# Codebook search with one fp32 matmul per unit, and depthwise taps as diagonal matmuls on TensorE

## The chip, the cores and the metric

The kernel runs on one core of a Trainium2 chip, in one launch. The metric is the device time in microseconds (us), lower is better. One core has TensorE (PE, matmuls into PSUM), VectorE (DVE), ScalarE (ACT), GpSimd (POOL) and SyncE (SP), which run their own instruction streams and wait for each other by semaphores. TensorE's clock is granted at one of two levels, 1.2 or 2.4 GHz; the profile shows which, as a share of full speed.

## The reference

The input x is 2 images of 128 channels and 48x48 pixels. Four layers each add to it: `x = x + layer(_gn(x))`, where `_gn` normalizes groups of 4 channels.

```python
# layer 0: guidance conv 3x3 -> softmax weights of 5x9 dilated taps -> 1x1 conv -> batch norm
# layer 1: nearest code of each pixel vector z among 8192 codes of 128 values
d = jnp.sum(z_flat ** 2, axis=1, keepdims=True) + jnp.sum(codebook ** 2, axis=1) - 2.0 * jnp.matmul(z_flat, codebook.T)
z_q = codebook[jnp.argmin(d, axis=1)]
# layer 2: depthwise 3x3 conv, its 9 taps of each image and channel computed from the pooled image
kern = jax.nn.relu(x.mean(axis=(2, 3)) @ Wk.T + bk)
out = lax.conv_general_dilated(xr, kern, ..., feature_group_count=b * c)
# layer 3: two deformable 3x3 convs (offset conv, gather of 4 corners of 9 taps, mix), each with group norm and relu
```

All in fp32. The channels lie on the 128 partitions.

## The kernel before

The program has these stages.

*Opening and guidance* (functions `Opening`, `guidance`): load x, normalize it into the padded image `xpad`, then for six rounds of 8 rows each a 3x3 conv on PE (`conv`, line 417), a softmax on DVE (lines 506 to 520), and transposes to and fro (`turn`, `turn_back`). Beside it, class `CodeSplit` loads the transposed codebook in 8 groups of 128x1024 fp32 through two buffers (SP, line 956), and POOL splits each into a bf16 high part (line 962) and a bf16 rest (line 964). The guidance block ends when all engines have done their part.

*Branches* (`branches`): the 45 dilated taps of layer 0, with DVE multiplying, PE and POOL adding.

*Between*: scalars of the two norms on DVE in a chain of small steps, then the first 512 pixels z of layer 1 as fp32 (line 886, DVE), as bf16 high (line 906, ACT) and as bf16 rest (line 888, DVE). PE starts the search when both are there. POOL then makes the other 4096 pixels, in fp32, high and rest (lines 917 to 934), and the second chunk of the search waits for it (`rest`, `DONE`).

*Search* (`search_steps`, `step`): 9 chunks of 512 pixels (n = 0 to 8), each in 4 steps (s), each of 16 units (k). A unit is the scores of 512 pixels against 128 codes: three bf16 matmuls of 128x512 into one PSUM bank (high x high, high codes x low z, low codes x high z; lines 1431 to 1433). Units 0 and 1 of a step are copied out by ACT with a bias (line 1593). Units 2 to 15 are taken by DVE, which keeps a running maximum (line 1864). The scores have 5 banks in turn (`SLOT`), so PE can be at most 4 to 6 units ahead of the engine that empties them. After units 9 and 11 PE transposes the running maxima of the step before (`turn`, line 1335), and once per chunk z (`turn_z`) and the chosen codes (`turn_zq`). For the chunk before, DVE finds the best blocks (`find`, `place_block`, at unit 12 and 14 of step 0 and at six units of step 1), POOL gathers candidates and multiplies, ACT sums, DVE picks, POOL fetches the codes and adds.

In the last three chunks further work is put between the units by the tables of the functions `lead`. At chunk 6 (`L0`), image 0 has its layer-1 result: DVE takes its moments (step 0, unit 10), PE makes the 9 tap weights of each channel (`pe_kernels`, line 220), ACT normalizes the image into `xpad` (`applied`), and DVE adds the nine taps to x with one full-image instruction each (`tap`, line 254) at nine units of steps 2 and 3, then takes the moments of the result. Chunks 7 and 8 prepare the first deformable job of image 0.

*First job* (`first_job`): the end of the search for the last chunk, then the same depthwise for image 1, with DVE doing 18 half-image taps (`half_tap`, line 264), nine for each half, with `weigh(0, 2, 4)` between the halves. In between, PE and ACT go on with tiles 2 to 4 of job 0, whose corners ACT multiplies (`product`, line 1634), while DVE's next tile is tile 5, behind `norm(1)`.

*Jobs*: 4 jobs (2 convs, 2 images) of 18 tiles of 128 pixels. For each tile POOL issues 9 indirect DMAs (`rows`, line 2076) that gather the corners into one of 5 buffers. `rows(T)` waits until PE has turned tile T-5 (`turn_done`). DVE weighs the corners (lines 1909 to 1919), PE turns (line 1458) and mixes (line 1469). The order on each engine is written out by hand, and every queue works in that order.

Of the kernel before, what the change touches and what calls it, by code (L numbers as in the profile page):

```python
# [15 lines left out]
P = 128  # L16
B, H, W = 2, 48, 48
# [7 lines left out]
ROWS = 8  # L25
# [164 lines left out]
class Depthwise:  # L190
# [5 lines left out]
    def __init__(self, tools, ctx, a, x, xpad, gm32):  # L196
# [10 lines left out]
        self.done = [tools.sem(ctx, "tap_done") for _ in range(B)]  # L207
# [34 lines left out]
    def dve_kernels(self, dve, b, ps):  # L242
        dve.wait_ge(self.kern_ready, b + 1)
        self.norm.chained(dve, dve.tensor_tensor(self.kern[:], ps[:, 2:2 + TAPS], self.bk[:], ALU.add))
        self.norm.chained(dve, dve.tensor_scalar(self.kern[:], self.kern[:], 0.0, None, ALU.max))
        dve.wait_ge(self.applied, b + 1)

    def tap(self, dve, b, k):
        v = self.xpad[:, b * PADDED:(b + 1) * PADDED].rearrange("p (r w) -> p r w", w=WP)
        v = v[:, k // 3:k // 3 + H, k % 3:k % 3 + W]  # L250
        xb = self.x[:, b, :].rearrange("p (r w) -> p r w", w=W)
        if k:
            dve.wait_ge(self.done[b], k)
        dve.scalar_tensor_tensor(xb, v, self.kern[:, k:k + 1], xb, ALU.mult, ALU.add).then_inc(self.done[b], 1)

    def half_tap(self, dve, b, h, k, sums):
        v = self.xpad[:, b * PADDED:(b + 1) * PADDED].rearrange("p (r w) -> p r w", w=WP)
        v = v[:, h * H // 2 + k // 3:h * H // 2 + k // 3 + H // 2, k % 3:k % 3 + W]
        xb = self.x[:, b, h * HW // 2:(h + 1) * HW // 2].rearrange("p (r w) -> p r w", w=W)
        sums = sums.rearrange("p (r w) -> p r w", w=W)  # L260
        n = TAPS * h + k
        if n:
            dve.wait_ge(self.done[b], n)
        dve.scalar_tensor_tensor(sums if k < TAPS - 1 else xb, v, self.kern[:, k:k + 1], sums if k else xb,
                                 ALU.mult, ALU.add).then_inc(self.done[b], 1)
# [101 lines left out]
def guidance(nc, tools, xpad, w_guide, ident, ident_b, a_sel, b_sel, wta, wtb, opening, beside):  # L367
# [5 lines left out]
    with ExitStack() as ctx:  # L373
# [387 lines left out]
def layer0(nc, tools, a, x, xpad, gm32, gm8, ident, codes, y, stats, xy, moments, gb, between):  # L761


    with ExitStack() as ctx:
# [3 lines left out]
        with ExitStack() as ctx:  # L768
# [9 lines left out]
            ch, cl, nc2, code_rows = codes  # L778
            with ExitStack() as parts:
                guidance(nc, tools, xpad, w_guide, ident, ident_b[:], (sel_a, id3a), (sel_b, id3b), wta, wtb,  # L780
                         Opening(tools, parts, x, xpad, gm32, moments, loads), CodeSplit(nc, tools, parts, a, ch, cl))
# [15 lines left out]
class Between:  # L797
# [6 lines left out]
    def __init__(self, tools, ctx, x, y, stats, xy, moments, gb, gm32):  # L804
# [14 lines left out]
        self.affine = tools.sem(ctx, "z_affine")  # L819
        self.high = tools.sem(ctx, "first_high")  # L820
        self.low = tools.sem(ctx, "first_low")
# [13 lines left out]
    def dve(self, dve, ps, each, z, zh, zl):  # L835
# [49 lines left out]
        dve.sem_inc(self.affine, 1)  # L885
        chain(dve.tensor_scalar(z, first, scale[:, 0:1], self.first_shift[:, 0:1], ALU.mult, ALU.add))
        dve.wait_ge(self.high, 1)
        dve.tensor_tensor(zl, z, zh, ALU.subtract).then_inc(self.low, 1)
# [3 lines left out]
    def pe(self, pe, ps):  # L892
# [4 lines left out]
        pe.wait_ge(self.high, 1)  # L897
        pe.wait_ge(self.low, 1)

    def act(self, act, zh):  # L900
# [4 lines left out]
        act.wait_ge(self.affine, 1)  # L905
        act.activation(zh, self.x[:, 0:self.FIRST], ACT.Identity, bias=self.first_shift[:, 0:1],
                       scale=self.scale[:, 0:1]).then_inc(self.high, 1)

    def pool(self, pool, early, places):
# [6 lines left out]
        pool.wait_ge(self.high, 1)  # L916
# [6 lines left out]
        for a, c, b in cuts:  # L923
            z, zh, zl = places(a, c)
            pool.tensor_scalar(z, x[:, a:c], self.scale[:, b:b + 1], self.shift[:, b:b + 1], ALU.mult, ALU.add)\
                .then_inc(rest, 1)
        pool.wait_ge(rest, 6)
        for a, c, b in cuts:
            z, zh, zl = places(a, c)
            pool.tensor_copy(zh, z).then_inc(rest, 1)  # L930
        pool.wait_ge(rest, 9)
        for a, c, b in cuts:
            z, zh, zl = places(a, c)
            pool.tensor_tensor(zl, z, zh, ALU.subtract).then_inc(rest, 1)

    DONE = 12


class CodeSplit:


    SLOTS = 2

    def __init__(self, nc, tools, ctx, a, ch, cl):
        self.a, self.ch, self.cl = a, ch, cl
        self.ct = tools.sb(ctx, "codes_t", [P, self.SLOTS, PER * P])
        self.ct_in = [tools.sem(ctx, "codes_t_in") for _ in range(self.SLOTS)]
        self.high = tools.sem(ctx, "high_ready")
        self.low = tools.sem(ctx, "low_ready")

    def sp(self, sp):
        for g in range(GROUPS):
            s = g % self.SLOTS
            if g >= self.SLOTS:
                sp.wait_ge(self.low, g - self.SLOTS + 1)
            sp.dma_start(self.ct[:, s, :], self.a["codes_t"][:, g, :]).then_inc(self.ct_in[s], 16)

    def pool(self, pool):
        for g in range(GROUPS):
            s = g % self.SLOTS  # L960
            pool.wait_ge(self.ct_in[s], 16 * (g // self.SLOTS + 1))
# [1272 lines left out]
```

## Time and profile before

| | us |
|---|---|
| median of 3 runs | 1657.97 (1655.91 to 1658.62) |
| the profiled execution, its own time | 1659.29 |
| its span, first to last instruction | 1657.5 |

| engine | busy us | share of the span |
|---|---|---|
| PE | 1207.6 | 73% |
| DVE | 1359.2 | 82% |
| ACT | 430.0 | 26% |
| POOL | 1009.7 | 61% |

The guidance fills the first 85 us of the span, the branches end at about 306, the search runs from 319 to 820, and the jobs fill the rest. The chain of work that ended last is mostly POOL (25% of the span, all in line 2076) and its issue time. In the rows below a start and a duration are in us; a grouped row ends with busy us, the mean of one in ns, and idle us before it; "x36" is the number of instructions merged into one row; a bracket behind a row is the idle time of the engine before it and what ended that. A duration of a matmul includes its latency, so the pace of a stream is read from distances of starts. An fp32 matmul has two instructions, and so two records, where a bf16 matmul has one.

### The profile page before, as it was taken

Reading aid. Unit: us, or ns where it says so; the run is one execution under the profiler, and the core shown is the slowest. Engines: PE = TensorE matmul, PEld = TensorE weight load, DVE = VectorE, ACT = ScalarE, POOL = GpSimd, SP = SyncE. Lnnn points to the kernel's source line nnn. Section 1 sums busy time; section 2 is a strip of 40 time slices with the busy share of each in tenths; the row PEclk is TensorE's granted clock in tenths of the full one; section 3 lists DMA queues with packets and bytes.
Section 4 is the critical chain, followed back from the end, with each engine's and each line's share of the span. In section 5 each row is a group of like instructions: output and inputs, shape, how many; then the busy total and the mean of one; then the engine's idle time right before and its main releaser. Section 6 shows DMA issues by size and latency. Waiting matters only on the chain. (4 is left out here: it accounts for less than half of the span.)

```text
span 1657.5 us, 19707 instructions
## 1 busy us (share of the span) xinstructions
PE 1207.6 (73%) x5997; PEld 747.5 (45%) x6040; DVE 1359.2 (82%) x1885; ACT 430.0 (26%) x1354; POOL 1009.7 (61%) x977
## 2 busy tenths in 40 slices
PE   5889989698889987689857685676665566555554
PEld 2455555354444444244336454544444444444443
DVE  5568678789999999989967889987887777797775
ACT  1241000124333443243457231221112212111111
POOL 6158578444333443235777677777777777777772
PEclk9889999899999999789978797697777778767677
DMA  4051000012111121053476796787877878777773
GB/s 168 13 166 40 1 0 0 15 31 58 53 43 34 46 58 39 20 153 107 142 225 201 216 288 208 211 267 229 247 209 228 248 229 247 211 232 212 208 210 99
DMA packets 111101, 232.64 MB, mean 140 GB/s; under 512 B 14676, under 2 KB 60500, under 8 KB 110748
## 3 DMA queue, kind: packets, MB, share of 16 engines
q0 software_dynamic: 58176, 191.30, 39.0%
q1 hardware_dynamic: 52828, 40.17, 7.7%
q8 instruction: 46, 0.75, 0.2%
q14 instruction: 51, 0.42, 0.1%
HBM read 205.15 MB, written 26.26 MB: 140 GB/s over the span
## 5 line engine op out<-in xcount | busy, mean ns | idle before, releaser
L2076 POOL DMA_INDIRECT code_region<-corners,lead_region x252 | 240.9, 956 | 77.9 <-issue 75.8
L1864 DVE SCALAR_TENSOR_TENSOR max_region<-score,nc,max_region 128x512 f32<-128x512 f32 x324 | 230.5, 740 | 28.4 <-PE score L1433 26.2
L742 POOL TENSOR_TENSOR prod_acc<-prod_acc,prod_pool 128x752 f32<-128x752 f32 (+8 forms) x112 | 151.8, 1355 | 98.1 <-DVE prod_pool L715 90.6
L2076 POOL DMA_INDIRECT early_region<-corners,lead_region x136 | 129.0, 948 | 41.3 <-issue 40.8
L1458 PE MATMUL score<-ident,code_region 128*128 128x128 f32 x540 | 96.9, 340 | 77.6 <-DVE code_region L1913 73.0
L2076 POOL DMA_INDIRECT max_region<-corners,lead_region x130 | 124.1, 955 | 39.6 <-issue 38.7
L2076 POOL DMA_INDIRECT late_region<-corners,lead_region x126 | 119.9, 951 | 44.6 <-issue 37.8
L1864 DVE SCALAR_TENSOR_TENSOR max_region<-lead_score,nc,max_region 128x512 f32<-128x512 f32 x180 | 132.2, 741 | 8.1 <-PE lead_score L1433 7.6
L1458 PEld LDWEIGHTS score<-ident,code_region 128*128 128x128 f32 x540 | 78.6, 176 | 94.8 <-DVE code_region L1913 87.5
L1991 POOL DMA_INDIRECT late_region<-code_rows,block_id x35 | 37.0, 1058 | 135.3 <-DVE block_id L1706 98.7
L664 PE MATMUL y_ps<-prod_pe,w_scale 128*128 128x384 f32 (+9 forms) x396 | 107.6, 397 | 0.0
L1909 DVE TENSOR_TENSOR lead_score<-lead_score,code_region 128x768 f32<-128x768 f32 x78 | 75.3, 966 | 37.0 <-DMA code_region<-corners,lead_region 33.8
L715 DVE TENSOR_TENSOR prod_pool<-spread,xpad 128x752 f32<-128x752 f32 (+8 forms) x112 | 81.9, 739 | 26.1 <-PE spread L641 25.3
L2003 POOL TENSOR_TENSOR late_region<-late_region 128x1032 f32<-128x1032 f32 x32 | 72.6, 2268 | 45.1 <-DMA late_region<-code_rows,block_id 44.4
L1530 ACT COPY max_region<-turn_ps 128x512 f32<-128x512 f32 x72 | 42.2, 586 | 202.3 <-PE turn_ps L1335 202.3
L1521 ACT ACTIVATE late_region<-late_region 128x129 f32<-128x129 f32 x280 | 82.5, 299 | 17.3 <-POOL late_region L2003 12.0
L641 PE MATMUL spread<-wta,sel_a 108*128 x352 | 74.7, 318 | 16.6 <-DVE prod_pool L715 6.6
L1641 ACT COPY code_region<-score 128x384 f32<-128x384 f32 x72 | 34.4, 478 | 191.2 <-PE score L1458 185.8
L1458 PE MATMUL score<-ident,early_region 128*128 128x128 f32 x292 | 50.2, 329 | 43.1 <-DVE early_region L1913 33.9
L1458 PE MATMUL score<-ident,late_region 128*128 128x128 f32 x252 | 48.6, 357 | 43.3 <-DVE late_region L1913 43.3
L715 DVE TENSOR_TENSOR prod_pe<-spread,xpad 128x768 f32<-128x768 f32 (+8 forms) x98 | 67.6, 698 | 14.8 <-PE spread L641 14.5
L1913 DVE TENSOR_TENSOR code_region<-lead_score,code_region 128x768 f32<-128x768 f32 x78 | 74.7, 957 | 2.7
(289 smaller groups left out, 3098.2 us busy)
## 6 DMA issues: line engine op xcount, KB each, us to landing
corners<-lead_region SPq DMA_DIRECT2D x72, 192.0 KB
corners<-lead_region SPq DMA_DIRECT2D x8, 576.0 KB
code_rows<-codes_n SPq DMA_DIRECT2D x8, 516.0 KB, 4.2
codes_t<-in_codes_t SPq DMA_DIRECT2D x8, 512.0 KB, 3.7
codes_n<-in_codes SPq DMA_DIRECT2D x8, 512.0 KB, 4.4
code_region<-corners,lead_region POOLq DMA_INDIRECT x252, 3.7
x<-in_x SPq DMA_DIRECT2D x2, 1152.0 KB, 6.3
out<-x SPq DMA_DIRECT2D x4, 576.0 KB, 3.3
```

Of the source, the lines that this page charges most:

```text
L641: mm = pe.matmul(to, sel[:, kk, :], v, start=True, stop=True)
L664: mm = pe.matmul(dst, w_scale[:, o["i"] + 1, :], src.rearrange("p (r w) -> p r w", r=rows), start=False, stop=last, skip_group_check=True)
L715: dve.tensor_tensor(to, w, v, ALU.mult).then_inc(prod_ready, 1)
L742: pool.tensor_tensor(to, to, v, ALU.add).then_inc(pooled, 1)
L1458: mm = pe.matmul(tps[g][:, k * P:(k + 1) * P], quad(T, 3 * g + k)[:, c * P:(c + 1) * P], ident, start=c == low, stop=c == CORNERS - 1, is_ ...
L1521: act.activation(v, v, ACT.Identity, accum_out=fine[:, u, j:j + 1]).then_inc(summed, 1)
L1530: act.copy(maxima[n % 2][:, :, g * P:(g + 1) * P], turn_ps[:]).then_inc(kept, 1)
L1864: dve.scalar_tensor_tensor(r, score[SLOT[k]], nc2[:, m:m + 1], r, ALU.add, ALU.max).then_inc(dve_took, 1)
L1909: return dve.tensor_tensor(upper_ps, bc(w[:, k, 0:2], P), q[:, k, 0:2], ALU.mult)
L1913: dve.tensor_tensor(q[:, k, 2:4], upper_ps, q[:, k, 2:4], ALU.add).then_inc(halved, 1)
L2003: pool.tensor_tensor(v, v, zb, ALU.mult).then_inc(multiplied, 1)
L2076: pool.indirect_dma_start(quad(T, k), None, table[j].rearrange("n s c -> n (s c)"), bass.IndirectOffsetOnAxis(index[j % B][:, at:at + 1], 0))\
```

## The change

1. The search has one fp32 matmul of 128x512 per unit in place of three bf16 ones. No high and low parts are made: `CodeLoad` loads the eight code groups straight into their place without POOL, `Between` makes z in fp32 alone, and POOL has 6 instructions in place of 12 before the second chunk.
2. The depthwise taps of both images are sums on PE: ACT makes nine diagonal 128x128 matrices from the tap weights (`act_diagonals`), and PE multiplies them with shifted windows of `xpad`, 9 matmuls of 128x384 per 8 rows, six such groups per image (`pe_taps`). DVE adds each result from PSUM to x.
3. For image 0 the groups of taps and their adds stand at units of steps 2 and 3 of chunk 6 (`TAPS_AT`, `ADDS_AT`). For image 1 PE does the groups of one half after `pe_kernels`, then tile 2, then those of the other half, then tiles 3 and 4; DVE has two adds of half an image.

```diff
+    def act_diagonals(self, act, b, ident, to):
+        act.wait_ge(self.kern_done, b + 1)
+        for k in range(TAPS):
+            act.activation(to[:, k * P:(k + 1) * P], ident, ACT.Identity, scale=self.kern[:, k:k + 1])\
+                .then_inc(self.diag_ready, 1)
+
+    def pe_taps(self, pe, b, r, diag, ps):
+        at = b * PADDED + r * (ROWS * WP)
+        for k in range(TAPS):
+            v = self.xpad[:, at + k // 3 * WP + k % 3:at + k // 3 * WP + k % 3 + ROWS * WP]
+            mm = pe.matmul(ps, diag[:, k * P:(k + 1) * P], v.rearrange("p (r w) -> p r w", w=WP)[:, :, 0:W],
+                           start=k == 0, stop=k == TAPS - 1)
+        return mm
...
-            beside.pool(pool)
...
-        pe.wait_ge(self.high, 1)
-        pe.wait_ge(self.low, 1)
-
-    def act(self, act, zh):
+        pe.wait_ge(self.first, 1)
+
+    def act(self, act):
...
+class CodeLoad:
...
     def sp(self, sp):
         for g in range(GROUPS):
...
+            sp.dma_start(self.codes[:, g, :], self.a["codes_t"][:, g, :]).then_inc(self.loaded, 16)
+        sp.wait_ge(self.loaded, 16 * GROUPS)
...
+    TAPS_AT = (0, 2, 1), (0, 2, 7), (0, 2, 13), (0, 3, 4), (0, 3, 9), (0, 3, 13)
+    ADDS_AT = (0, 2, 4), (0, 2, 10), (0, 3, 2), (0, 3, 7), (0, 3, 12), (0, 3, 15)
...
-                    pe.matmul(o, ch[g][:, w], high, start=True, stop=False)
-                    pe.matmul(o, ch[g][:, w], low_, start=False, stop=False)
-                    pe.matmul(o, cl[g][:, w], high, start=False, stop=True).then_inc(score_ready, 1)
+                    pe.matmul(o, codes_t[:, g, w], chunk_of(z_early, z_late, n), start=True, stop=True)\
+                        .then_inc(score_ready, 1)
...
                 depthwise.pe_kernels(pe, 1, dps)
-                for T in range(2, 5):
+                taps(0)
+                tile(0, 2 // TPC, 2 % TPC)
+                taps(1)
+                for T in range(3, 5):
                     tile(0, T // TPC, T % TPC)
...
                 depthwise.act_norm(act, 1)
+                depthwise.act_diagonals(act, 1, ident, diag1)
...
-                for t in range(2 * TAPS):
-                    if t == TAPS:
-                        weigh(0, 2, 4)
-                    depthwise.half_tap(dve, 1, t // TAPS, t % TAPS, tap_sums)
+                weigh(0, 2, 4)
+                for h in range(2):
+                    xh = x[:, 1, HALVES[h]].rearrange("p (c n) -> p c n", n=CH)
+                    dve.wait_ge(depthwise.tapped, NCH + h + 1)
+                    dve.tensor_tensor(xh, tap_sums, xh, ALU.add).then_inc(depthwise.done[1], 1)
```

`taps(h)` on PE waits for all nine diagonals, and for h = 1 for DVE's first add. Each group for image 0 waits in the same way for the add of the group before.

## Rows read from the trace of the kernel before

**Rows 1.** Timeline of PE in chunk 2 of the search: start, duration, engine, line, operation.

```profile
400.36 0.38 PE L1431 MATMUL lead_score<-early_region,code_region 128*128 128x512 bf16 x1
400.58 0.38 PE L1432 MATMUL lead_score<-early_region,code_region 128*128 128x512 bf16 x1
400.80 0.38 PE L1433 MATMUL lead_score<-early_region,code_region 128*128 128x512 bf16 x1
401.01 0.60 PE L1335 MATMUL turn_ps<-ident,max_region 128*128 128x128 f32 x4
401.45 0.38 PE L1431 MATMUL lead_score<-early_region,code_region 128*128 128x512 bf16 x1
```

**Rows 2.** PE timeline of fp32 matmuls, 256 and 384 columns; the latter's group.

```profile
872.45 1.46 PE L1469 MATMUL turn_ps<-max_region 128*128 128x256 f32 x6
...
304.56 1.48 PE L664 MATMUL y_ps<-prod_acc,w_scale 128*128 128x384 f32 x4
...
L664 PE MATMUL y_ps<-prod_acc,w_scale 128*128 128x384 f32 x96 | 35.9, 496 | 0.0
```

**Rows 3.** Timeline of ACT: its first units of steps 0, 1, 2 of chunk 2 and of chunk 3.

```profile
416.67 1.27 ACT L1593 ACTIVATE max_region<-lead_score,nc 128x512 f32<-128x512 f32 x2 [3.20 <-PE lead_score L1433]
428.34 1.28 ACT L1593 ACTIVATE max_region<-lead_score,nc 128x512 f32<-128x512 f32 x2 [2.06 <-PE lead_score L1433]
444.29 1.27 ACT L1593 ACTIVATE max_region<-lead_score,nc 128x512 f32<-128x512 f32 x2 [2.73 <-PE lead_score L1433]
...
467.75 1.27 ACT L1593 ACTIVATE max_region<-lead_score,nc 128x512 f32<-128x512 f32 x2 [3.15 <-PE lead_score L1433]
```

**Rows 4.** DVE: two units in the timeline; the finds of one chunk, grouped by line.

```profile
816.07 1.40 DVE L1864 SCALAR_TENSOR_TENSOR max_region<-score,nc,max_region 128x512 f32<-128x512 f32 x2
...
L1701 DVE MAX8 best<-max_region 128x8 f32<-128x1024 f32 x4 | 4.9, 1218 | 0.0
```

**Rows 5.** Chunk 0, chunk 6, its steps 2 and 3, chunk 7, chunk 8: busy time by engine.

```profile
320.50:365.55 45.05, 44.84 (x214) 21.87 (x217) 37.74 (x56) 8.76 (x14) 29.90 (x13) 0.98 0.11 29
621.01:696.82 75.81, 56.76 (x248) 28.11 (x252) 71.56 (x106) 22.26 (x83) 25.24 (x22) 0.87 0.12 32
655.86:696.82 40.96, 27.68 (x114) 12.75 (x116) 40.12 (x50) 11.91 (x56) 15.90 (x14) 0.84 0.12 33
696.82:765.28 68.46, 58.18 (x273) 27.95 (x277) 63.65 (x116) 27.74 (x92) 20.84 (x22) 0.89 0.36 104
765.28:820.20 54.92, 48.76 (x249) 23.32 (x252) 49.95 (x95) 20.46 (x82) 39.92 (x42) 1.00 0.45 133
```

The columns are window, its length, busy us and instructions of PE, weight loads, DVE, ACT and POOL, the granted clock, the DMA share and GB/s.

**Rows 6.** Line 254, the taps of image 0: min/median/max in ns, first and last start.

```profile
L254 DVE SCALAR_TENSOR_TENSOR x<-xpad,kern,x x9: 2605/2609/3879, 658.6 to 699.0; 128x2304 f32<-128x2304 f32 x9
```

**Rows 7.** Timeline of PE in the guidance.

```profile
42.09 0.26 PE L435 MATMUL wa_ps<-ident_b,w_split 128*108 128x128 bf16 x1 [3.79 <-DVE w_split L520]
...
44.99 8.05 PE L417 MATMUL g_ps<-xpad,w_guide 128*64 128x384 f32 x36
...
55.42 6.03 PE L417 MATMUL g_ps<-xpad,w_guide 128*64 128x384 f32 x36
```

**Rows 8.** Timeline ahead of the search, DVE.

```profile
318.18 0.69 DVE L888 TENSOR_TENSOR early_region<-early_region 128x512 bf16<-128x512 f32 x1 [0.32 <-ACT early_region L906]
```

**Rows 9.** Timelines of the first job: DVE, ACT, PE and POOL.

```profile
881.33 0.17 DVE L245 TENSOR_SCALAR kern<-kern 128x9 f32<-128x9 f32 x1
...
884.16 3.61 ACT L1634 ACTIVATE code_region<-code_region,lead_region 128x128 f32<-128x128 f32 x12
...
905.11 4.09 PE L1458 MATMUL score<-ident,max_region 128*128 128x128 f32 x36
...
914.06 0.59 PE L149 MATMUL z_ps<-n_mean_var,gm 128*128 128x2 f32 x2 [4.86 <-DVEq L144]
...
927.87 0.94 POOL L2076 DMA_INDIRECT late_region<-corners,lead_region  x1 [6.48 <-PE score L1458]
```

**Rows 10.** Waits of POOL from 822 us to the end: total us, times, longest.

```profile
POOL late_region L2076 <- PE score L1458: 6.8, 2, 6.5
```

More of the change, by code:

```diff
@@ L206, in __init__ @@
         self.applied = tools.sem(ctx, "applied")
-        self.done = [tools.sem(ctx, "tap_done") for _ in range(B)]
+        self.kern_done = tools.sem(ctx, "kernels_done")
+        self.diag_ready = tools.sem(ctx, "diagonals_ready")
+        self.tapped = tools.sem(ctx, "taps_summed")
+        self.done = [tools.sem(ctx, "taps_added") for _ in range(B)]
     def sp(self, sp):
@@ L243, in dve_kernels @@
         dve.wait_ge(self.kern_ready, b + 1)
+        if b:
+            dve.wait_ge(self.diag_ready, TAPS * b)
         self.norm.chained(dve, dve.tensor_tensor(self.kern[:], ps[:, 2:2 + TAPS], self.bk[:], ALU.add))
[L245 to L265, printed above, removed]
+        dve.tensor_scalar(self.kern[:], self.kern[:], 0.0, None, ALU.max).then_inc(self.kern_done, 1)
+    def act_diagonals(self, act, b, ident, to):
[10 more added lines that the diff above has]
+        return mm
 class Opening:
@@ L818, in __init__ @@
         self.group_rooted = tools.sem(ctx, "x_group_rooted")
-        self.affine = tools.sem(ctx, "z_affine")
-        self.high = tools.sem(ctx, "first_high")
-        self.low = tools.sem(ctx, "first_low")
+        self.first = tools.sem(ctx, "first_ready")
         self.shifts = tools.sem(ctx, "z_shifts")
@@ L884, in dve @@
         chain(dve.tensor_tensor(self.first_shift[:], self.first_shift[:], scale, ALU.mult))
[L885 to L888, printed above, removed]
+        dve.tensor_scalar(z, first, scale[:, 0:1], self.first_shift[:, 0:1], ALU.mult, ALU.add).then_inc(self.first, 1)
         chain(dve.scalar_tensor_tensor(self.shift[:], gmean, -1.0, scale, ALU.mult, ALU.mult))
@@ L1034, in code_views @@
 def code_views(region):
[L1036 to L1041 removed]
+    return region[:, 0:CODES].rearrange("p (g n) -> p g n", g=GROUPS)
 def finale(nc, tools, a, code_rows, x, xpad, ident, gm32, gm8, nc2, depthwise, between, places, out):
@@ L1404, in lead @@
                     depthwise.pe_kernels(pe, 0, lead_ps)
+                for r, when in enumerate(TAPS_AT):
+                    if at == when:
+                        pe.wait_ge(depthwise.applied, 1)
+                        pe.wait_ge(depthwise.diag_ready, TAPS)
+                        if r:
+                            pe.wait_ge(depthwise.done[0], r)
+                        depthwise.pe_taps(pe, 0, r, diag0, lead_ps[:, 0:CH]).then_inc(depthwise.tapped, 1)
                 if at == (1, 0, 3):
@@ L1471, in tile, with taps @@
                     mm.then_inc(mixed, 1)
+            def taps(h):
+                pe.wait_ge(pos_ready, 1 + NCH)
+                pe.wait_ge(depthwise.applied, 2)
+                pe.wait_ge(depthwise.diag_ready, 2 * TAPS)
+                if h:
+                    pe.wait_ge(depthwise.done[1], h)
+                for r in range(NCH // 2):
+                    mm = depthwise.pe_taps(pe, 1, h * NCH // 2 + r, diag1, tap_sums[:, r, :])
+                mm.then_inc(depthwise.tapped, 1)
             def first_job():
@@ L1686, in _ @@
             act.sem_inc(y_saved, 1)
-            between.act(act, zh_early[:, 0:PX])
+            between.act(act)
             search_steps(step)
@@ L1820, in lead @@
                     depthwise.dve_kernels(dve, 0, lead_ps)
-                for t, when in enumerate(((0, 2, 2), (0, 2, 3), (0, 2, 8), (0, 2, 13), (0, 2, 15),
-                                          (0, 3, 10), (0, 3, 11), (0, 3, 13), (0, 3, 14))):
+                for r, when in enumerate(ADDS_AT):
                     if at == when:
-                        depthwise.tap(dve, 0, t)
+                        xc_ = x[:, 0, r * CH:(r + 1) * CH]
+                        dve.wait_ge(depthwise.tapped, r + 1)
+                        dve.tensor_tensor(xc_, lead_ps[:, 0:CH], xc_, ALU.add).then_inc(depthwise.done[0], 1)
                 if at == (0, 3, 15):
-                    dve.wait_ge(depthwise.done[0], TAPS)
+                    dve.wait_ge(depthwise.done[0], NCH)
                     norm_.dve_moments(dve, x[:, 0, :])
@@ L1876, in norm @@
                 if j < 0:
-                    dve.wait_ge(depthwise.done[b], 2 * TAPS)
+                    dve.wait_ge(depthwise.done[b], 2)
                     norm_.dve_moments(dve, x[:, b, :])
```

73 lines of the change are left out of this document (19 added, 54 removed).

## The prediction

> **What bounds the kernel now.** I read the page's busy tenths first to see the stages, then for the search the starts of the steps and the paces of PE and DVE, then for the jobs the waits of POOL and the timelines around image 1's depthwise. Four stages matter.
>
> In chunk 0 of the search PE sets the pace. Three bf16 matmuls start 0.215 us apart, so a unit costs 0.647 us, and four transposes 0.44 us [rows 1]. A step of 16 units with two such turns is 16 x 0.647 + 0.88 = 11.23 us of PE, and chunk 0 took 45.05 us, 11.26 a step, with PE busy all but 0.2 us [rows 5]. In chunks 1 to 5 a chunk is 51.1 us (11.67 in step 0, 15.95 in step 1, 23.46 in the other two) [rows 3], while PE alone, with z and code transposes (0.88), would need 4 x 11.23 + 0.88 = 45.8. The missing 5.3 us lie at step 1: there DVE has its finds, 1.22 us each [rows 4], beside units that it takes at 0.66 us (two in 1.40, one's latency being 0.74) [rows 4]. So PE is 90% of the bound, and DVE the rest. Chunks 6 and 7 took 75.8 and 68.5 us with DVE busy 71.6 and 63.7 [rows 5]: there DVE's extra work is the bound.
>
> After the search POOL issues one gather every 1.25 us to the end. From 822 us on its waits for another engine in the main group sum to 6.8 us, nearly all one wait of 6.5 [rows 10]. So whatever holds POOL up in the first job moves the end by as much, and what speeds up PE or DVE there is worth at most those 6.5 us.
>
> **The change part by part.**
>
> *Unit of the search.* The trace has no fp32 matmul of 512 columns. With 256 columns six records take 1.46 us; with 0.38 for the last one's duration (that of the 512-column bf16 matmul [rows 1], which streams as many cycles) they are 0.216 apart, two records a matmul, 0.43 each. With 384 columns four records take 1.48: (1.48 - 0.50) / 3 = 0.33 apart, 0.65 a matmul [rows 2]. Both are four cycles a column at 2.4 GHz, with a new weight load each time that hides. So 512 columns cost 2 x 0.43 = 0.857 us, against 0.647: +0.21 us a unit. From 384 columns the same price comes to 0.65 x 512 / 384 = 0.87; I take 0.857, as the 256 columns are the cleaner stream, and keep 0.87 for the range. A step becomes 13.7 + 0.9 = 14.6 us of PE.
>
> The Trainium skill (TensorE: Matmul & The Clock Gate, Back-to-back issue gap) gives about 131 ns per 512-column matmul as the sustained pace in a stream with weight loads. The trace disagrees: 215 ns in exactly such a stream [rows 1]. By the page an fp32 unit of four passes would be an estimated 0.52 us, less than DVE's 0.66, and the first rival below would win.
>
> *Chunk 0:* 4 x 14.6 = 58.4, +13.4 us. POOL's six saved instructions there are worth nothing: it has a whole chunk for them.
>
> *Chunks 1 to 5:* PE needs 4 x 14.6 + 0.9 = 59.2 us. DVE's burst lasts from unit 12 of step 0 to unit 13 of step 1: 16 units x 0.66 and 8 finds at some 1.15 net, 19.8 us. PE's 18 units in it were 12.5 us and become 16.3. The difference falls from 7.3 to 3.5. The banks let PE run ahead some 2.0 us now (7.3 - 5.3), some 2.6 at slower units, so 1 us of stall remains; I take 1.2 (bounds 0 and today's 5.3). A chunk becomes 60.4, +9.3, five times +46.5 us.
>
> *Chunk 6:* DVE loses nine taps of 2.61 us (one 3.88) [rows 6], 24.8 us, and gets six adds of 384 columns. The trace has no such add; a unit's 0.66 for 512 columns [rows 4] bounds one from above and nothing from below, I take 0.55, 3.3 us, which decides nothing while PE is the bound. PE gets 54 matmuls of 0.65 to 0.66, 35.6 us. So the bound moves to PE: 59.2 + 35.6 + 2.5 (norm, kernels) = 97.3 us. The finds, moments and small steps of steps 0 and 1 keep DVE ahead as bound for a while; by the same reckoning as above PE stalls there some 4.4 us. 101.7 against 75.8: +25.9. Of that, the 41.0 us of steps 2 and 3 [rows 5] become 64 to 65. The diagonals are nine ACT instructions of 0.30 us (twelve in 3.61) [rows 9] in ACT's idle time; PE's first group can wait for them a us or so.
>
> *Chunk 7:* DVE no longer enters it late by two taps and the moments, and PE does 59.2 plus some 5 us of conv and transposes, with 1.3 of stall: 65.5 against 68.5, -3.0. *Chunk 8:* 59.2 + 2.6 + 1.8 = 63.6 against 54.9, +8.7. Together the search gets 13.4 + 46.5 + 25.9 - 3.0 + 8.7 = +91.5 us.
>
> *Guidance.* Without POOL's split DVE's first softmax rounds are no longer slowed, and PE's idle 3.8 us before the first turn back goes; the conv behind it, 8.05 us at a partly low clock where later ones take 6.03, and the turns beside it (1.0 us) run at full clock [rows 7]: 3.8 + 2.0 + 1.0 = -6.8. The later rounds are PE's own pace. The bounds are 0 and -9. The code loads now follow at once on the queue behind all others, which cost nothing by their place.
>
> *Before the search.* The rest of z and its wait are gone: -1.1 us (0.69 + 0.32 and a signal) [rows 8].
>
> *First job.* The tap weights are ready at 881.5 [rows 9]. ACT's diagonals take 2.7 us, PE's 27 matmuls 17.8, so tile 2 starts at 902 instead of 881, or 904 when the first matmuls run at the low clock after the wait. With tile 2's 4.1 us and 27 more matmuls taps(1) ends at 926. DVE's last add and the moments follow within some 5 us, 931; in the kernel before PE made that norm at 914.1 [rows 9]. But PE now stands before tiles 3 and 4. Tile 3 is turned by 930, tile 4 waits for ACT's products, which interleave with tile 3's copies (three times 3.61 [rows 9] and a copy of about half a us, from 926.5, so 939), and norm(1) follows on PE at 940.3: +26. DVE's tile 5 and then `rows(10)` on POOL, which started at 927.9 [rows 9], follow at that distance: 954. POOL's rows(8) and rows(9) in between wait too, but inside this. DVE loses its 18 half taps and gains nothing, since it waits. +26 us (bounds +14, if ACT's products were done early, and +45, if all 54 matmuls ran at half clock).
>
> *POOL's queue at the end of the search.* DVE's last picks lie 8 units before the end, which is 1.7 us longer now, so POOL has its fetches behind it that much earlier: -1.7.
>
> Sum against the profiled execution's 1659.3: 91.5 - 6.8 - 1.1 + 26 - 1.7 = +107.9, 1767.2. That execution lies 1.3 above the median of the runs, so I give 1766.
>
> **The rivals.**
>
> *DVE stays the bound of the search (faster).* It decides at the price of a unit: below (51.1 - 4.4) / 64 = 0.73 us, 0.365 a record, chunks 1 to 5 don't grow. For it speaks only that DVE is busy 82% of the span; against it, both fp32 widths in rows 2. At 0.52 a unit and taps scaled alike (0.39), the search loses some 20 us in chunk 6 and 5 in chunk 7, and the first job grows by some 8: 1659.3 - 7.9 - 20 - 5 + 8 = 1634. Chance 3%.
>
> *The stalls don't shrink.* If the finds cost PE the full 5.3 us a chunk with the longer units as well, chunks 1 to 5 get 4.1 each, chunks 6 and 8 some 3: +27, 1793. Against it: banks that hold longer units give more slack, not less. Chance 12%.
>
> *The clock falls in the taps.* In the first job PE waits before each half and the granted clock can be half for some of it, and around chunk 6's hand-overs too. Half of the 54 matmuls at 1.2 GHz cost 18 us more: 1784. Speaking for it: matmuls in streams with waits ran at the low clock in chunk 6 (0.84 mean) [rows 5]. Against: the taps are dense. Chance 10%.
>
> *The first job's delay is absorbed.* If POOL could catch up, +26 would vanish: 1740. Rows 10 show no slack to catch up with. Chance 6%.
>
> **How the numbers follow.** Forecast 69%, the others 3, 12, 10 and 6. The predicted time is the forecast's. Its own uncertainty is +-12: 3 for guidance, 6 for chunks 6 and 7, 6 for the stalls, 8 for the first job, and +8 at 0.87 us a unit (576 x 0.013). The range takes in the absorbed delay and the shrinking that fails, 1740 to 1793. A measurement of this kernel can tell 0.2%, 3.3 us, from no change. All cases but the first lie far above that: faster 0.03, same 0.01, slower 0.96.
>
> **What would show it.** In the changed kernel's trace: records of line 1431's successor 0.43 us apart; steps of 14.6 us in chunk 0; PE busy over 95% in chunks 1 to 5 with chunks of 60 us; chunk 6 near 102 us with DVE busy under 55; PE without the 3.8 us gap in the guidance, which ends near 78; norm(1) about 26 us later after the search's end than now, and POOL waiting there some 25 us more, with no other new wait. The prediction is wrong if a unit costs under 0.73 us, if chunks 1 to 5 come out at 64 or more, or if POOL regains time after the first job.

## The result and the profile after

| | before | after |
|---|---|---|
| median | 1658.3 us (1655.91 to 1658.77, 4 runs) | 1785.62 us (1783.28 to 1788.28, 4 runs) |
| the profiled execution, its own time | 1659.29 | 1783.28 |
| its span | 1657.5 | 1781.5 |

The ratio is 1.0768, with a 95% interval of 1.0755 to 1.0781: 7.7% slower, 127 us, where 108 were forecast. 1785.6 lies inside the range. The two spans differ by 124.0 us, and these are split below.

The page's first part for the kernel after, then the slices of 44.5 us each (busy tenths; PEclk is the granted clock):

```profile
PE 1386.8 (78%) x5680; PEld 834.3 (47%) x5680; DVE 1333.5 (75%) x1865; ACT 436.8 (25%) x1371; POOL 969.0 (54%) x955
...
PE   6899897999999999999984968666654765655554
...
DVE  4478677687888888368885178998788877878776
...
PEclk9899998999999999999997989768786887767666
```

PE gained 179 us of busy time, DVE lost 26. PE is at 9 from slice 8 to slice 20, nearly the whole search; DVE has a 3 (slice 17, in chunk 6, whose taps it gave away) and a 1 (slice 23, where it waits for PE in the first job).

The pace of a unit, in PE's timeline of chunk 0, as rows 1 showed it for before:

```profile
317.47 1.02 PE L1398 MATMUL score<-early_region,code_region 128*128 128x512 f32 x2
318.32 1.02 PE L1398 MATMUL lead_score<-early_region,code_region 128*128 128x512 f32 x2
319.18 1.02 PE L1398 MATMUL score<-early_region,code_region 128*128 128x512 f32 x2
```

A unit, two records, starts every 0.855 us, so 0.43 a record, twice the 0.216 that rows 2 gave for 256 columns. The stages in windows, with the columns of rows 5: chunk 0 (opened 1.1 us ahead of ACT's first unit, from which the table below counts it), chunk 1, chunk 6, its steps 2 and 3, chunk 7, chunk 8 with what follows its last score:

```profile
312.00:371.88 59.88, 59.88 (x155) 27.61 (x154) 42.04 (x56) 9.01 (x14) 18.55 (x7) 0.97 0.08 22
371.88:432.74 60.86, 59.74 (x169) 27.98 (x168) 51.07 (x81) 20.14 (x81) 18.56 (x20) 1.00 0.14 40
676.27:781.26 104.99, 100.73 (x297) 52.28 (x296) 57.93 (x106) 25.06 (x92) 20.89 (x22) 0.97 0.08 23
716.27:781.26 64.99, 64.21 (x191) 34.30 (x192) 23.91 (x47) 11.98 (x57) 10.33 (x12) 1.00 0.07 20
781.26:850.52 69.26, 65.44 (x213) 31.07 (x212) 59.24 (x112) 28.04 (x92) 20.86 (x22) 1.00 0.36 103
850.52:919.00 68.48, 64.55 (x200) 30.27 (x199) 55.24 (x95) 21.21 (x83) 43.21 (x46) 0.98 0.41 119
```

PE is busy all but 1.1 us of chunk 1 and all but 0.8 us of chunk 6's steps 2 and 3, where DVE has only 23.9 us of work left in 65. With the distances between ACT's first units (as rows 3), E for the end of the last score, and "jobs" for all that follows E in the span, the search of each kernel that was run comes out so (us):

| kernel | search starts | chunk 0 | 1 to 5, each | 6 | 7 | 8 | E | jobs |
|---|---|---|---|---|---|---|---|---|
| before | 319.4 | 45.1 | 51.1 | 75.8 | 68.5 | 54.5 | 819.7 | 837.8 |
| after | 310.9 | 58.8 | 60.9 | 105.0 | 69.3 | 66.2 | 916.8 | 864.7 |
| fp32 search alone | 310.4 | 58.8 | 60.9 | 78.2 | 77.5 | 66.3 | 897.7 | 840.8 |
| image 0's taps on DVE | 309.1 | 59.1 | 60.9 | 78.2 | 75.8 | 66.3 | 895.0 | 868.0 |
| image 1's taps on DVE | 310.0 | 58.7 | 60.9 | 105.0 | 69.7 | 66.6 | 916.5 | 840.1 |
| bf16 search, taps on PE | 320.0 | 45.1 | 51.1 | 95.9 | 65.3 | 54.4 | 837.8 | 866.3 |
| four bf16 a unit | 315.6 | 58.6 | 61.0 | 76.4 | 76.4 | 66.2 | 900.1 | 836.3 |
| two bf16 a unit | 319.6 | 37.6 | 47.7 | 73.4 | 68.2 | 52.5 | 790.9 | 843.0 |
| pauses in the split | 310.5 | 45.4 | 51.1 | 74.3 | 70.4 | 54.3 | 811.8 | 838.1 |
| tiles between the taps | 312.1 | 58.9 | 60.9 | 105.0 | 69.8 | 66.3 | 918.8 | 864.2 |
| half of the taps on each | 311.5 | 58.8 | 60.9 | 105.0 | 69.7 | 68.3 | 919.9 | 860.8 |
| the same, tile 2 first | 310.9 | 58.8 | 60.9 | 105.0 | 69.7 | 66.2 | 917.2 | 846.2 |

The first two lines split the 124.0 us: -8.5 ahead of the search, +13.7 in chunk 0, +49.0 in chunks 1 to 5, +29.2, +0.8 and +11.7 in chunks 6, 7 and 8, +26.9 in the jobs, and 1.2 at the search's start and in rounding. At that start, after a wait of 3.0 us, the kernel after ran its first records 0.89 us apart instead of 0.43, at a granted clock of 0.50 (the kernel before began at the low clock too, with its shorter unit):

```profile
310.95 3.78 PE L1398 MATMUL lead_score<-early_region,code_region 128*128 128x512 f32 x4 [2.98 <-DVE early_region L881]
```

Each line of the table is one execution, and its parts scatter. The jobs take 836.3 to 843.0 us in the six kernels with image 1's taps on DVE and 864.2 to 868.0 in the four with all of them on PE, so a difference of 2 or 3 us in the jobs of two kernels has no cause that these runs show.

### The profile page after: what moved, and what is told of

The parts are those of the page before. It is cut to its first block and busy times, and to the rows that moved or that the text cites. A ratio compares the mean times of both kernels' runs of the same rounds, so it can differ in the third digit from the quotient of the medians.

```text
span 1781.5 us, 19014 instructions
## 1 busy us (share of the span) xinstructions
PE 1386.8 (78%) x5680; PEld 834.3 (47%) x5680; DVE 1333.5 (75%) x1865; ACT 436.8 (25%) x1371; POOL 969.0 (54%) x955
## 3 DMA queue, kind: packets, MB, share of 16 engines
q0 software_dynamic: 58176, 191.30, 36.5%
## 5 line engine op out<-in xcount | busy, mean ns | idle before, releaser
L1846 DVE SCALAR_TENSOR_TENSOR max_region<-score,nc,max_region 128x512 f32<-128x512 f32 x324 | 238.2, 746 | 104.3 <-PE score L1398 89.1
L1398 PE MATMUL score<-early_region,code_region 128*128 128x512 f32 x360 | 174.9, 595 | 0.0
L1398 PE MATMUL lead_score<-early_region,code_region 128*128 128x512 f32 x280 | 142.0, 601 | 7.4 <-DVE max_region L1846 4.5
L1398 PE MATMUL score<-late_region,code_region 128*128 128x512 f32 x288 | 144.0, 607 | 1.5 <-DVE max_region L1846 1.5
L1398 PE MATMUL lead_score<-late_region,code_region 128*128 128x512 f32 x224 | 113.2, 599 | 3.1 <-DVE max_region L1846 3.1
L1398 PEld LDWEIGHTS score<-early_region,code_region 128*128 128x128 f32 x360 | 66.3, 191 | 77.2 <-issue 67.0
## 6 DMA issues: line engine op xcount, KB each, us to landing
code_region<-in_codes_t SPq DMA_DIRECT2D x8, 512.0 KB, 10.1
```

Of the source, the lines that this page charges most:

```text
L1398: pe.matmul(o, codes_t[:, g, w], chunk_of(z_early, z_late, n), start=True, stop=True)\
L1846: dve.scalar_tensor_tensor(r, score[SLOT[k]], nc2[:, m:m + 1], r, ALU.add, ALU.max).then_inc(dve_took, 1)
```

## The experiments

### The three parts one by one

*The search alone.* The kernel before with part 1 of the change; the taps of both images stay on DVE.

> The changed kernel with the depthwise taps of both images on DVE again, as in the kernel before; only the search unit, the code loads and what lies between are changed. Theory (a unit costs PE 0.857 us, and each stage goes by its own bound): guidance and before the search -8 us, chunk 0 +14, chunks 1 to 5 +49, chunk 6 only some +3 since DVE's taps bound it as before, chunk 7 +3, chunk 8 +12, first job 0: 1658.3 + 73 = 1731. Rival (PE's slower unit adds to DVE's taps, the two don't overlap in chunk 6): chunk 6 gets the full 13.5 as well, 1742.

Measured: 1739.1 us, ratio 1.0485 (1.0467 to 1.0503). So the fp32 unit with all that belongs to it is 81 of the 124 us of span. That is 8 us above the theory and near the rival's 1742, but the rival asked for 13.5 us more in chunk 6, which got 2.4; it is chunk 7 that got 9.0 where 3 were expected (see below).

*Image 0's taps back on DVE*, and in a second kernel *image 1's*, from the kernel after:

```diff
-                        xc_ = x[:, 0, r * CH:(r + 1) * CH]
-                        dve.wait_ge(depthwise.tapped, r + 1)
-                        dve.tensor_tensor(xc_, lead_ps[:, 0:CH], xc_, ALU.add).then_inc(depthwise.done[0], 1)
+                        depthwise.tap(dve, 0, t)
...
-                taps(0)
-                tile(0, 2 // TPC, 2 % TPC)
-                taps(1)
-                for T in range(3, 5):
+                for T in range(2, 5):
```

> The changed kernel with the taps of image 0 alone on DVE again. Theory: chunk 6 falls from 105 to some 79 us and chunk 7 rises by 2, the first job stays as in the changed kernel: 1760. Rival (the low clock after waits, and not the 54 matmuls, makes chunk 6 long): chunk 6 stays over 90 us, 1772 or more.

> The changed kernel with the taps of image 1 alone on DVE again. Theory: the first job gives back the 24 us by which POOL's tenth group of gathers comes later after the search, POOL's wait of 33 us falls to under 7: 1761. Rival (POOL's wait has another cause, such as its earlier arrival): the wait stays over 20 us, 1775 or more.

Measured: 1764.8 us, 1.0642 (1.0619 to 1.0666), and 1757.3 us, 1.0597 (1.0571 to 1.0623). By the spans (1763.0 and 1756.6) image 0's taps on PE cost 18.5 us and image 1's 24.9. With 81.0 for the search that makes 124.4 of 124.0: the parts add up, though not as finely as this looks. By the ratios, against some 1658 us, they are 80, 21 and 28 us, 130 of 127. The table shows where: image 0's taps cost 26.8 us in chunk 6 and give 6.5 back in chunk 7, and 3.3 in the jobs, within the scatter named above; image 1's cost 24.6 in the jobs and nothing before. POOL's longest wait for a turn fell from 33.2 to 4.3 us with image 1's taps on DVE, as expected.

*The taps alone*, beside the bf16 search, tell whether they cost because the search had become PE-bound:

> The kernel before with the taps of both images on PE as in the change (diagonals of image 0 in the place of y of image 0, which is free then); the search unit stays three bf16 matmuls. Theory: chunk 6 goes from 75.8 to some 87 us (PE 45.8 + 35.6 + 2.5 and 3 of stall), chunk 7 -4, first job +24 to +27: 1692. Rival (with cheap units the taps hide in PE's idle time in chunk 6, 19 us there): chunk 6 at 76 or less, 1680.

Measured: 1705.9 us, 1.0273 (1.0254 to 1.0292), 14 us above what was expected, 9 of them in chunk 6. The taps cost no less with bf16 units, 46.6 us of span against 43.0 beside the fp32 ones: +20.1 in chunk 6, -3.2 in chunk 7, +28.5 in the jobs. The windows of chunk 6, and of its steps 2 and 3 with the taps:

```profile
621.90:717.80 95.90, 87.93 (x361) 47.16 (x360) 56.30 (x106) 24.78 (x92) 20.89 (x22) 0.96 0.09 26
658.00:717.00 59.00, 56.94 (x217) 31.17 (x218) 22.80 (x47) 12.79 (x60) 10.71 (x14) 1.00 0.08 23
```

DVE was 40.1 of 41.0 us busy there [rows 5], and is 22.8 of 59.0 now: nine DVE taps (24.8 us [rows 6]) became some 35 us of matmuls (27 of them take 17.58 us in image 1's rows below) on an engine that was busy 27.7 us with its own in these steps, at a granted clock of 0.84 [rows 5]. At the paces of rows 1 its own work is 22.5 us, and 22.5 + 35 is close to the 59.0 of the second window. The expected 87 us had set PE's whole chunk against one bound. But steps 0 and 1 stay DVE's (36.7 us, 34.9 before), and only steps 2 and 3 turn PE's (59.2): a chunk is the sum of its steps' maxima, not the maximum of its sums.

### Is it the price of the unit, or fp32 itself?

The unit of the kernel before, with one more bf16 matmul, and with one fewer:

```diff
-                    pe.matmul(o, cl[g][:, w], high, start=False, stop=True).then_inc(score_ready, 1)
+                    pe.matmul(o, cl[g][:, w], high, start=False, stop=False)
+                    pe.matmul(o, cl[g][:, w], low_, start=False, stop=True).then_inc(score_ready, 1)
```

> The kernel before with a fourth bf16 matmul per unit (low codes x low z). A unit costs PE 0.863 us, as much as the fp32 matmul's 0.857. Theory (only the price of the unit counts): the search grows as in fp32_search_only, without the 8 us gained ahead of it: 1740. Rival (fp32 has costs of its own, such as its longer weight loads of 190 ns): under 1730.

> The kernel before with two bf16 matmuls per unit; the product of the codes' low part with z's high part is left out. A unit costs PE 0.43 us, so DVE bounds all of the search. Theory (PE sets only chunk 0 and the parts of chunks 1 to 5 outside the finds): chunk 0 -6 us, chunks 1 to 5 -2 each, chunk 8 -2: 1640. Rival (PE was the bound of the whole search): -0.2 us per unit, 1560.

Measured: 1741.9 us, 1.0494 (1.0476 to 1.0512), and 1634.4 us, 0.9842 (0.9822 to 0.9862). PE's timeline with four:

```profile
396.09 0.38 PE L1431 MATMUL score<-early_region,code_region 128*128 128x512 bf16 x1
...
396.95 0.38 PE L1431 MATMUL lead_score<-early_region,code_region 128*128 128x512 bf16 x1
```

0.86 us a unit, and the table's lines of four bf16 and of the fp32 search agree within 0.2 us in chunks 0 to 5 and 8 (chunk 6 differs by 1.8, chunk 7 by 1.1). So in the search nothing of the fp32 matmul but its length counts, and its weight loads cost nothing that those of bf16 don't. The Trainium skill (FP8 and Floating Point Precision, TensorE Precision Notes) gives a true fp32 matmul four passes through the array; here the trace agrees, as one fp32 unit takes as long as four bf16 matmuls. With two matmuls (0.43 us) the chunks 1 to 5 stop at 47.7 us, where PE alone would need some 32 (64 x 0.43, and 4.4 of turns at rows 1's 0.44 each): DVE is busy all of that chunk,

```profile
362.00:409.00 47.00, 37.21 (x166) 15.52 (x164) 46.99 (x81) 19.94 (x81) 20.38 (x22) 0.93 0.19 51
```

So by this window a still faster unit would not bring chunks 1 to 5 below some 47.7, from 51.1. Three matmuls stood near the crossing of both engines, and the change went past it: 3.4 us a chunk were to be had, 9.8 were lost.

### The guidance without the split beside it

The kernel before, with POOL's split of the codes made to wait for DVE's softmax rounds:

```diff
         for g in range(GROUPS):
             s = g % self.SLOTS
+            if g > 2:
+                pool.wait_ge(split_done, g - 1)
```

> The kernel before, where POOL splits the code groups 3 to 7 only after the softmax rounds 0 to 4 are done on DVE, one group after each. Theory (in the guidance DVE's first round, slowed beside POOL, lets PE wait 3.8 us and lowers its clock): the guidance ends 6.8 us earlier as in the changed kernel, 1651.5. Rival (the gain came with the fewer or earlier loads, or the barrier): no change, 1658.

Measured: 1652.6 us, 0.9956 (0.9942 to 0.9969), 0.4% faster than the kernel before and the fastest here that computes all three products. DVE's first softmax round in the kernel before:

```profile
34.52 1.21 DVE L513 TENSOR_TENSOR g_res<-g_exp,g_den 128x270 f32<-128x270 f32 x1
35.76 2.21 DVE L517 CAST w_split<-g_res 128x270 bf16<-128x270 f32 x1
```

and with the pauses, POOL waiting for that round until 36.6 us:

```profile
34.09 0.44 DVE L513 TENSOR_TENSOR g_res<-g_exp,g_den 128x270 f32<-128x270 f32 x1
34.57 0.40 DVE L517 CAST w_split<-g_res 128x270 bf16<-128x270 f32 x1
```

The same two instructions take 3.42 us beside POOL's split and 0.84 alone. In the kernel with four bf16 matmuls, whose guidance is that of the kernel before, POOL happened to wait for a DMA at that moment: the two took 0.84 us (the three behind them were slow), PE's wait was 1.9 us instead of 3.8, and the guidance ended at 82.53 with no change made to it. The Trainium skill (SBUF — State Buffer, SBUF: two separate sides) names a port pair that DVE and GpSimd lock for a whole instruction in some forms; these rows fit that. The guidance's end came 6.2 us sooner (79.28 for 85.44; 78.68 in the kernel after). Most of the change's gain ahead of the search thus needs neither fp32 codes nor the loads without a split.

### The first job: amount, order or cover?

In the kernel after PE stands so in the first job (timeline; E is at 916.8):

```profile
978.76 20.38 PE L262 MATMUL lead_score<-xpad,wk 128*128 128x384 f32 x54 [3.33 <-ACT wk L255]
...
1002.90 17.58 PE L262 MATMUL lead_score<-xpad,wk 128*128 128x384 f32 x54
1020.33 4.09 PE L1424 MATMUL score<-ident,code_region 128*128 128x128 f32 x36
...
1030.12 1.56 PE L1435 MATMUL turn_ps<-late_region,max_region 128*128 128x256 f32 x6 [2.31 <-ACT late_region L1621]
1031.52 4.09 PE L1424 MATMUL score<-ident,max_region 128*128 128x128 f32 x36
1035.45 0.28 PE L149 MATMUL z_ps<-n_mean_var,gm 128*128 128x2 f32 x2
```

and POOL:

```profile
1025.21 0.95 POOL L2059 DMA_INDIRECT code_region<-corners,lead_region  x1 [33.17 <-PE score L1424]
...
1048.95 0.95 POOL L2059 DMA_INDIRECT late_region<-corners,lead_region  x1 [1.42 <-PE score L1424]
```

`rows(8)` waited 33.2 us for the turn of tile 3. First I took this for a matter of order, and put tile 2 ahead of all taps and tile 3 between the halves:

```diff
-                taps(0)
                 tile(0, 2 // TPC, 2 % TPC)
+                taps(0)
+                tile(0, 3 // TPC, 3 % TPC)
                 taps(1)
-                for T in range(3, 5):
-                    tile(0, T // TPC, T % TPC)
+                tile(0, 4 // TPC, 4 % TPC)
```

> The changed kernel with PE's order in the first job changed: tile 2, taps of one half, tile 3, taps of the other half, tile 4. Same work. Theory (the order decides: ACT's products for tiles 3 and 4, 12 us each, then run beside the taps, and tile 2 fills the wait for the diagonals): norm(1) on PE comes 8 us earlier and POOL's first long wait falls from 33 to about 11 us, 1777.6. Rival (the amount of PE work decides): no change, 1785.

Measured: 1781.7 us, 1.0738 (1.0718 to 1.0759), 3.9 us less; the interval just overlaps that of the kernel after. norm(1) came 118.6 us behind E instead of 118.7. POOL's one wait had become two:

```profile
1006.82 0.95 POOL L2059 DMA_INDIRECT code_region<-corners,lead_region  x1 [12.66 <-PE score L1424]
...
1037.12 0.95 POOL L2059 DMA_INDIRECT max_region<-corners,lead_region  x1 [19.29 <-PE score L1424]
```

So I formed the theory that the amount of PE's work decides. It was tried by taking one of the two groups of 27 matmuls away, DVE doing that half in x itself meanwhile:

```diff
-                taps(1)
...
+                for k in range(TAPS):
+                    depthwise.half_in_place(dve, 1, k)
+                xh = x[:, 1, HALVES[0]].rearrange("p (c n) -> p c n", n=CH)
+                dve.wait_ge(depthwise.tapped, NCH + 1)
+                dve.tensor_tensor(xh, tap_sums, xh, ALU.add).then_inc(depthwise.done[1], 1)
```

> The changed kernel, but only half 0 of image 1 has its taps on TensorE; half 1 is nine in-place DVE taps of half an image, made while PE works on half 0, and the second group of 27 matmuls is gone. Theory (the amount of PE work in the first job sets its delay, not its place): PE's 27 matmuls of the second half took 17.58 us in the changed kernel, all of it ahead of tiles 3 and 4; DVE's nine taps of 1.42 us (12.8) lie beside the 20.4 us of the first half. So norm(1) comes on PE some 101 us after the last score (118.7 in the changed kernel, 94 before), POOL's wait of 33.2 us becomes some 16, and the time is 1785.6 - 17.6 = 1768, ratio 1.066. Rival (what counts is that PE waits for kernels and diagonals at all before tiles 2 to 4, and that ACT's products come late): under 8 us are saved, 1778 or more. Rival (DVE's nine taps hold up its first add and the moments): 1775.

Measured: 1778.7 us, 1.0709 (1.0694 to 1.0723). DVE's nine taps did hide (13.05 us, then 6.75 of idle), but of the 17.6 us taken from PE norm(1) gained only 6.5 (112.2 behind E). That theory fell too. PE's timeline of this kernel shows what came up in their place:

```profile
984.11 19.71 PE L270 MATMUL lead_score<-xpad,wk 128*128 128x384 f32 x54 [3.33 <-ACT wk L263]
...
1009.22 1.53 PE L1432 MATMUL score<-ident,code_region 128*128 128x128 f32 x12 [1.46 <-ACT code_region L1621]
1013.10 1.53 PE L1432 MATMUL score<-ident,code_region 128*128 128x128 f32 x12 [2.35 <-ACT code_region L1621]
1016.98 1.53 PE L1432 MATMUL score<-ident,code_region 128*128 128x128 f32 x12 [2.35 <-ACT code_region L1621]
...
1025.10 2.25 PE L1443 MATMUL turn_ps<-late_region,max_region 128*128 128x256 f32 x6 [2.31 <-ACT late_region L1628]
1027.15 5.12 PE L1432 MATMUL score<-ident,max_region 128*128 128x128 f32 x36
```

PE now waits for ACT's products of tile 3. ACT makes them between the copies of tile 2, three times 3.6 us and a copy, 11.7 us in all, and can begin only once tile 2 is turned. In the kernel after they lay under the second group of taps. So the last experiment keeps the work and moves tile 2 alone, one line, so that the products lie under the group that is left (the diff is against the kernel with half of the taps on each):

```diff
-                taps(0)
                 tile(0, 2 // TPC, 2 % TPC)
+                taps(0)
```

> As the kernel with half of image 1's taps on DVE, but PE does tile 2 before the taps instead of behind them. In that kernel PE lost one group of 17.58 us and norm(1) came only 6.5 us sooner (112.2 us behind the last score, 118.7 in the changed kernel), because ACT's products of tile 3, three times 3.9 us with the copies of tile 2 between them, had lain under that group and were now bare: tile 3's turns waited 6.2 us for them and the mixing behind 3.7. Theory (what decides is PE's taps and ACT's products laid end to end or over each other): with tile 2 first, ACT's 11.7 us lie under the one group of 17.6, so rows(8) goes on some 11 to 12 us sooner, norm(1) comes on PE some 99 to 101 us behind the last score, POOL's rows(10) at about 113 (132.2 in the changed kernel), and the time is 1765 to 1769, ratio 1.065. Rival (the amount of PE's work alone decides, and the products don't matter): no change, 1778.

Measured: 1763.6 us, 1.0629 (1.0614 to 1.0643), 15.0 us less than without the move. (The spans differ by 17.3: 14.6 lie in the jobs, and 2.1 in chunk 8, whose step 1 was 3 us longer in the profiled execution of the kernel without the move, though the code of the search is the same.) PE's and ACT's timelines:

```profile
977.56 3.50 PE L1432 MATMUL score<-ident,lead_region 128*128 128x128 f32 x16
...
983.08 17.58 PE L270 MATMUL lead_score<-xpad,wk 128*128 128x384 f32 x54
1000.50 4.09 PE L1432 MATMUL score<-ident,code_region 128*128 128x128 f32 x36
...
1017.29 0.28 PE L149 MATMUL z_ps<-n_mean_var,gm 128*128 128x2 f32 x2
```

```profile
980.80 0.46 ACT L1628 COPY code_region<-score 128x384 f32<-128x384 f32 x1
981.15 3.62 ACT L1621 ACTIVATE code_region<-code_region,lead_region 128x128 f32<-128x128 f32 x12
```

The products run beside the taps, tile 3's 36 turns go through in one row of 4.09 us without a wait, and norm(1) is at 100.1 us behind E, 12.1 sooner. Not all of this is the products. By the rows, some 7 us are waits for ACT that are gone (1.46 + 2.35 + 2.35, and 0.9 in the mixing behind). Some 4 are another effect of the same line: tile 2 now fills the 3.33 us in which PE waited for the diagonals, and the taps run at full clock (17.58 us for 19.71), while tile 2's first 16 turns take 3.50 us, where they took 1.91 behind the taps. No run separates the two, and 2.5 of the 14.6 us in the jobs lie behind norm(1) without a cause shown. So three things decide: how much PE has to do, whether ACT's products lie under it, and what PE does while it waits for the diagonals. This also answers the kernel with tiles between the taps: its second tile step uncovered the products of tile 4, whose wait PE took ahead of taps(1), while in the kernel after it took the same wait behind them. PE's 54 matmuls and the one uncovered set of products stand in the sum in either order. That kernel too filled the wait for the diagonals, but its second group then took 19.17 us and tile 2's first turns 3.57, so most of that was lost again.

## Why the prediction was right, and where it was short

The sign, the order of the parts and the range held; the sum was 16 us short (124.0 against 107.9). Step by step:

*The unit.* Said 0.857 us from the 256-column rows of rows 2; measured 0.855. The upper bound from 384 columns, 0.87, wasn't needed. Chunk 0 was to cost +13.4 and cost +13.7.

*DVE stays the bound* was the rival at 3%, and the 131 ns a matmul that the Trainium skill gives (TensorE: Matmul & The Clock Gate, Back-to-back issue gap) would have made it win. Four bf16 matmuls in 0.86 us are 215 ns each again, and DVE did not stay the bound.

*Chunks 1 to 5.* Said 60.4 each, measured 60.9. The stall was right (1.2 said, 60.86 less 59.74 busy, 1.1, measured), so the rival that the stalls don't shrink is refuted: they fell from 5.3. PE's own work was set at 59.2 and is 59.7. Half a us, five times: 2.5 us.

*Chunk 6.* Said +25.9, measured +29.2. Steps 2 and 3 were right (64 to 65 said, 64.99 measured). The term that was short is steps 0 and 1: 40.0 us, where 101.7 less 64.5 leaves 37.2. PE's idle time in them is 3.5 us, less than the 4.4 of the prediction; its busy time is 36.5 where the prediction had 32.6 (two steps of 14.6, 0.9 and 2.5). The window of step 1 and the row in it:

```profile
692.63:716.27 23.64, 20.98 (x60) 10.58 (x58) 20.90 (x39) 9.94 (x32) 8.03 (x8) 0.86 0.17 47
```

```profile
699.94 3.06 PE L223 MATMUL lead_score<-pooled,wk 128*128 128x1 f32 x18 [2.26 <-DVEq L243]
```

PE waits 2.3 us for DVE there, 2.7 us in the step in all, and the granted clock is 0.86 over the step, so the wait is followed by work at the lower level. I had counted the wait and not the clock behind it. One sign did not hold: DVE was busy 57.9 us in chunk 6, and under 55 was said. Its units now come one by one, 0.75 us each, where two in a row had taken 1.40; that decides nothing while PE is the bound.

*Chunk 7.* Said -3.0, measured +0.8, so the sign was wrong. PE's work is 65.4 us where I had 64.2, and the idle time 3.8 where I had 1.3; 2.5 of that are in step 0. Its step 1 is PE's alone:

```profile
799.82:818.36 18.54, 18.54 (x74) 8.81 (x73) 17.09 (x25) 7.06 (x25) 7.98 (x8) 1.00 0.77 226
```

18.54 of 18.54 us: 14.6 of units and their two turns, 3.9 of transposes and convs for the coming job. In the kernel before they lay beside DVE's longer work, and I had taken them as a total rather than where they stand. What I had right is the benefit from taps on PE: with the taps on DVE and the fp32 unit, chunk 7 is 77.5 us (75.8 in the other such kernel), 9 more than before, where I had expected 3 more in that experiment. DVE then enters chunk 7 late, PE waits for it, and the clock over those 26 us is 0.87:

```profile
752.00:778.00 26.00, 18.82 (x49) 8.75 (x50) 22.69 (x37) 7.35 (x10) 2.53 (x2) 0.87 0.00 0
```

*Chunk 8.* Said +8.7, measured +11.7 (0.4 of that is only the end that is taken: 820.2 in the prediction's window, 819.7 here). The rest is half waits, half the term of chunk 6: PE is idle 3.2 us, 2.0 in step 1 and 1.2 in step 2, where 1.8 were set, and busy 63.1 where 61.8 were. In step 1 PE waits 2.0 us for DVE, and the six records behind take 4.43 us, where at 0.43 each, with 0.59 for the last one's duration, they would take 5 x 0.43 + 0.59 = 2.7:

```profile
880.71 1.13 PE L1398 MATMUL lead_score<-late_region,code_region 128*128 128x512 f32 x2 [1.99 <-DVE max_region L1846]
881.67 4.43 PE L1398 MATMUL score<-late_region,code_region 128*128 128x512 f32 x6
```

*Guidance and what lies ahead of the search.* Said -7.9, measured -8.5: the guidance ends at 78.68 for 85.44, -6.8 as said, and 1.7 follow instead of 1.1. That second term is not resolved: from the guidance's end to the search's start it is 231.3 to 234.0 us in the five kernels with the split and 231.0 to 232.8 in the seven without.

*The first job.* Said tile 2 at +82 to 84 behind E, taps(1) done at +106, norm(1) at +120.6, `rows(10)` at +134; measured 82.2, 103.7, 118.7 and 132.2, where before had 94.3 and 108.1 [rows 9]. The 26 us are there, 24.1 at `rows(10)`, and 2.8 come later, which is within the scatter of the jobs; the -1.7 for POOL's queue does not show in the total, and no run here shows it. What the prediction did not see is why: it counted ACT's products of tile 4, rightly, but not that those of tile 3 were under the taps. The total was right for that, since what is covered costs nothing. The rival of an absorbed delay is refuted. The rival that the clock falls in the taps is refuted at its size: the first group took 20.38 us and the second 17.58, so 2.8 us were lost in the job, at a granted clock of 0.86 over the first group, where it asked for 18; the taps of chunk 6 ran at 1.00. That the time landed at that rival's figure (1784) was chance.

Of the 16 us that were missing, chunks 6 to 8 are 10.1, chunks 1 to 5 2.5, the jobs 2.6, and 0.9 the rest (0.3 in chunk 0, 1.2 at the search's start and in rounding, -0.6 ahead of it).

## What to carry to other kernels

Price a matmul by the records it has and the pace of such records in the trace, and compare that with what the taking engine needs for the same unit: three bf16 matmuls here stood at the crossing of PE and DVE, and an fp32 one is past it. Where two engines share the bound, add up the steps' maxima, each with the work that stands in that step, and allow for a low clock behind PE's waits: 1.7 us were lost behind one wait in chunk 8. When work is moved onto an engine that others wait for, ask what lay beside the idle time it now fills and what was covered by the work it replaces: one line's order was worth 15 us here, once the amount had gone down. With the full amount the one other order that was run gave 3.9 us, hardly clear of the noise.

## What the runs showed of the hardware

- An fp32 matmul of 128x512 is two records of 0.43 us, the same as four bf16 ones of 0.215, and of 128x384 0.65 us, with a new weight load each time.
- A 128x270 cast on DVE took 2.21 us while POOL ran its elementwise instructions, 0.40 us without.
- Some waits of PE of 2 to 3 us were followed by slow stretches, with a granted clock below 1: 1.7 us lost in chunk 8's step 1, 2.8 us at the start of image 1's taps. Others were not: behind the same wait of 2.31 us, 36 turns took 4.09 us in the kernel after and 5.12 in the one with half of the taps on each. Their length varies for the same code: step 1 of chunk 8 took 18.6 us in most kernels with this search, and 21.6 in the one with half of the taps on each. The runs don't tell what sets it.
- 27 fp32 matmuls of 128x384 with diagonal weights take 17.58 us at full clock. DVE's nine half-image taps of the same size take 13.05 us: for a depthwise 3x3 of 128 channels in fp32 DVE is the faster engine, and PE is worth it only in time that PE has to spare.
